# Second self-attention: one pass over both batches, fp32 scores of two heads in the two row halves of TensorE

## The reference, cut to what matters

```python
N_HEADS, D_HEAD = 16, 64
h = _layernorm(x, ln1_g, ln1_b)
q = (h @ sa_wq).reshape(B, S, 16, 64)
k = (h @ sa_wk).reshape(B, T, 16, 64)
v = (h @ sa_wv).reshape(B, T, 16, 64)
attn = softmax(einsum('bihd,bjhd->bhij', q, k) * 64 ** -0.5)
x = einsum('bhij,bjhd->bihd', attn, v).reshape(B, S, 1024) @ sa_wo + sa_bo + x
```

## Time and profile before

| | |
|---|---|
| Median of 3 runs | 2552.8 us (2549.9 to 2553.42) |
| The profiled execution, its own time | 2548.93 us |
| Its span, first to last instruction | 2547.2 us |
| Granted TensorE clock, mean over the span | 0.934 of full |
| TensorE busy | 2199.0 us (86%) |
| VectorE busy | 1323.1 us (52%) |
| ScalarE busy | 877.3 us (34%) |
| GpSimd busy | 501.7 us (20%) |
| Second self-attention with its projection, 941.9 to 1998.2 us | 1056.3 us |

### The profile page before, as it was taken

How to read it: one execution, slowest core, us unless ns; L and a number is a source line. 1 busy time by engine, 2 the same in 40 slices (tenths; PEclk the granted TensorE clock), 3 DMA queues, 4 the chain that set the end, 5 groups by cost and what they waited for, 6 DMA issues and landing times. The chain is left out here.

```text
span 2547.2 us, 27612 instructions
## 1 busy us (share of the span) xinstructions
PE 2199.0 (86%) x10154; PEld 1359.7 (53%) x10154; DVE 1323.1 (52%) x2139; ACT 877.3 (34%) x1349; POOL 501.7 (20%) x391
## 2 busy tenths in 40 slices
PE   5389997798999948999999989999998788898987
PEld 3234434386866834444444545444444677585766
DVE  4776652625244336666666256666664124535353
ACT  3046663322323222444444304444444132212221
POOL 3201100013123120332222202232323001202020
PEclk9699998799999977999999979999999799999989
DMA  3724302000000011000000011000000440000000
GB/s 110 112 34 52 44 12 77 15 1 1 1 0 0 1 31 40 24 24 23 23 24 18 1 37 39 24 23 23 23 17 1 117 117 1 0 9 8 0 9 8
DMA packets 62286, 71.34 MB, mean 28 GB/s; under 512 B 15386, under 2 KB 49180, under 8 KB 61892
## 3 DMA queue, kind: packets, MB, share of 16 engines
q1 hardware_dynamic: 62180, 69.92, 12.5%
HBM read 44.39 MB, written 8.73 MB: 21 GB/s over the span
## 5 line engine op out<-in xcount | busy, mean ns | idle before, releaser
L1694 DVE TENSOR_REDUCE pmax_b<-ring_b 128x1 f32<-128x512 f32 x512 | 346.7, 689 | 162.0 <-PE ring_b L1578 159.7
L1746 ACT ACTIVATE pr_b<-sc_b 128x1024 f32<-128x1024 f32 x256 | 261.7, 1023 | 352.8 <-PE sc_b L1598 352.8
L1656 POOL TENSOR_TENSOR sum_b<-sum_b,pr_b 128x1024 f32<-128x1024 f32 x96 | 228.3, 2378 | 247.3 <-ACT pr_b L1746 247.3
L1578 PE MATMUL ring_b<-k_hh_b,q_hl_b 128*128 128x512 f32 x512 | 241.2, 492 | 34.9 <-DVE pmax_b L1694 12.3
L1608 PE MATMUL o_b<-pr_b,v_b 128*64 128x512 f32 x1024 | 270.0, 617 | 0.0
L1578 PEld LDWEIGHTS ring_b<-k_hh_b,q_hl_b 128*128 128x128 f32 x512 | 102.2, 202 | 233.7 <-DVE pmax_b L1694 139.9
L504 ACT ACTIVATE probs<-s 128x512 f32<-128x512 f32 (+1 forms) x304 | 163.2, 575 | 159.8 <-PE s L414 112.9
L1596 PE MATMUL sc_b<-q_hl_b,k_hh_b 128*128 128x512 f32 x512 | 208.1, 406 | 4.7 <-ACT pr_b L1746 2.5
L1598 PE MATMUL sc_b<-q_m_b,k_l_b 65*128 65x512 f32 x512 | 204.8, 400 | 0.0
L982 PE MATMUL c_ps<-vw,c_pT 128*128 128x256 f32 x640 | 165.5, 419 | 22.2 <-ACT c_pT L1046 22.2
L982 PEld LDWEIGHTS c_ps<-vw,c_pT 128*128 128x128 f32 x640 | 132.6, 213 | 47.4 <-ACT c_pT L1046 25.4
(11 more groups left out here) (275 smaller groups left out, 3439.7 us busy)
## 6 DMA issues: line engine op xcount, KB each, us to landing
q_m_b<-q_hl_b SPq DMA_DIRECT2D x32, 256.0 KB, 3.5
k_hh_b<-k_hh_b SPq DMA_DIRECT2D x32, 256.0 KB, 3.4
qk_dram<-qk_parts SPq DMA_DIRECT2D x32, 192.0 KB, 2.8
q_stack<-qk_dram SPq DMA_DIRECT2D x48, 128.0 KB
k_stack<-qk_dram SPq DMA_DIRECT2D x48, 128.0 KB
x<-in_x SPq DMA_DIRECT2D x1, 2048.0 KB, 8.3
mlp_w<-in_L_xattn_mlp_w SPq DMA_DIRECT2D x2, 1024.0 KB, 8.5
wq_b<-in_L_xattn_sa_wq SPq DMA_DIRECT2D x16, 128.0 KB, 2.2
```

The costliest lines, as they stand in the source:

```text
L1578: te.matmul(ring[:, halves[i % 2]], q_hl[new][j][:, t * P:(t + 1) * P], k_hh[new][j][:, halves[half]], start=True, stop=True).then_inc(s1_ ...
L1656: engine.tensor_tensor(out=total[j][:], in0=other[:], in1=probs[j][kt % KEPT][:], op=ALU.add).then_inc(done, 1)
L1694: dve.tensor_reduce(part_max[:, half, j, t:t + 1], ring[:, halves[i % 2]], AX.X, ALU.max).then_inc(s1_max, 1)
L1746: act.activation(probs[j][kt % KEPT][:], s2[u % 2][:], ACT.Exp).then_inc(exp_made, 1)
```

## The change

`part_attention2` is called once and goes over 16 pairs, 8 of each batch, in one Block that holds the output projection too.

- **Scores.** A unit u = 8 * half + kt (0 to 15) is one tile of 128 keys, one half of 512 queries, and both heads. For each head there is a bf16 matmul (`picks` by `shift`) that puts the negated maximum into PSUM, and one fp32 matmul of contraction 64 (`kf` by `qf`). Head 0's operands lie on partitions 0 to 63, head 1's on 64 to 127. The splits of q and k and the DMA copies are gone. The maximum is carried as three bf16 parts (`split`, five small instructions of VectorE), and VectorE rounds q and k to F32R for the maxima (four casts a pair).
- **Maxima.** 32 F32R matmuls of contraction 64 a pair (`maxima`), heads in turn, in a ring of three PSUM tensors.
- **Order of TensorE.** Two units; then what `aside` gives for these two (projections in u = 0 to 2, four maxima for each u from 3 to 10, the turn at u = 11); then two steps of values, two units behind.
- **Sums.** All 14 additions of a pair are on GpSimd. The sums over partitions (`den`) use a slot of `s2`, twice a pair; ScalarE copies the values out (`copy_out`) and inverts (`invert`), in two halves.
- **Output projection.** Batch 0's eight tiles go behind units 12 to 15 of pairs 8 and 9 (`outs`), batch 1's behind the last pair. All weights are loaded at the start, in four chunks.

```diff
-def part_attention2(nc, e, A, b):
+def part_attention2(nc, e, A):
...
+        PAIRS, U, KEPT, SLOTS, CHUNKS, RING = 16, 16, 5, 12, 4, 3
+        S1 = 32
+        w = [sb(f"sa_w{n}", [P, KC, 1024]) for n in "qkv"]
+        wo_w, wo_brep = sb("wo_w", [P, 8, C]), sb("wo_brep", [P, C])
+        aT = sb("aT2", [P, SLOTS, T])
+        qf, kf = [sb(f"q_full{i}", [P, T]) for i in two], [sb(f"k_full{i}", [P, T]) for i in two]
+        qr, kr = sb("q_round", [P, T], F32R), sb("k_round", [P, T], F32R)
+        v = [sb(f"v_pair{i}", [P, TB, P]) for i in two]
+        probs = [sb(f"pr{i}", [P, 2, 512]) for i in range(KEPT)]
+        total, rden, raw = ([sb(f"{name}{h}", shape) for h in two] for name, shape in (
+            ("total", [P, 2, 512]), ("rden2_", [P, 512]), ("raw2_", [P, 512])))
+        part_max, row_max = sb("pmax", [P, 2, TB, 2]), sb("rmax", [P, 2, TB])
+        top, top_rest = sb("top2", [16, P]), sb("top2_rest", [16, P])
+        top_parts = [sb(f"top2_parts{i}", [16, 3, P], BF16) for i in two]
+        shift = [sb(f"shift{i}", [P, T], BF16) for i in two]
+        picks = sb("picks", [P, P], BF16)
+        ring = [ctx.enter_context(nc.psum_tensor(f"ring2_{i}", [P, 512], F32)) for i in range(RING)]
+        s2 = [ctx.enter_context(nc.psum_tensor(f"sc{i}", [P, 2, 512], F32)) for i in two]
+        o = ctx.enter_context(nc.psum_tensor("o2", [P, 512], F32))
...
+        head = (slice(0, 64), slice(64, P))
+        halves = (slice(0, 512), slice(512, T))
...
+        DEN_AT = 1
+        LAG = 2
...
+        def aside(u):
+            return (range(2 * u, 2 * u + 2) if u < 3 else (), range(4 * (u - 3), 4 * (u - 2)) if 3 <= u < 11 else (),
+                    u == 11)
+        def outs(n, u):
+            return (u - 12 + 4 * (n - 8),) if n in (8, 9) and u >= 12 else ()
...
+            for i in range(CHUNKS):
+                cols = slice(256 * i, 256 * i + 256)
+                for tile, n in zip(w, ("sa_wq", "sa_wk", "sa_wv")):
+                    sp.dma_start(tile[:, :, cols], A["L2_xattn_" + n].rearrange("(k p) f -> p k f", p=P)[:, :, cols]
+                                 ).then_inc(w_in[i], 16)
+            sp.dma_start(wo_w[:], A["L2_xattn_sa_wo"].rearrange("(k p) c -> p k c", p=P)).then_inc(wo_in, 16)
+            sp.dma_start(wo_brep[:], A["L2_xattn_sa_bo"].partition_broadcast(P)).then_inc(wo_in, 16)
...
+            for n in range(PAIRS):
+                sp.wait_ge(top_made, 5 * (n + 1))
+                sp.dma_start(e.top_dram[n % 2, :, 0:16].rearrange("s r q -> r s q"), top_parts[n % 2][:]
+                             ).then_inc(top_out, 16)
+                sp.wait_ge(top_out, 16 * (n + 1))
...
+                    sp.dma_start(shift[n % 2][64 * j:64 * j + 3], e.top_dram[n % 2, :, 8 * j:8 * j + 8].rearrange(
+                        "s t q -> s (t q)")).then_inc(shift_in, 16)
...
+            def project(n, i):
+                b, p, dst, half = n // 8, n % 8, ring[i % RING], i % 2
...
+                if i == 2 and n:
+                    te.wait_ge(top_made, 5 * (n - 1) + 1)
+                if i >= RING:
+                    te.wait_ge(kept, 6 * n + i - RING + 1)
...
+                if i < 4:
+                    for k in range(KC):
+                        ins = te.matmul(dst[:], w[i // 2][:, k, p * P:(p + 1) * P],
+                                        tokens_of(512 * half, 512 * half + 512)[:, k], start=k == 0, stop=k == KC - 1)
...
+            def maxima(n, i):
+                t, half, j = i // 4, i // 2 % 2, i % 2
+                if i < RING:
+                    te.wait_ge(kept, 6 * n + 4 + i)
+                    te.wait_ge(rounded, 4 * n + 4)
+                else:
+                    te.wait_ge(s1_free, S1 * n + i - RING + 1)
+                te.matmul(ring[i % RING][:], qr[head[j], t * P:(t + 1) * P], kr[head[j], halves[half]], start=True,
+                          stop=True).then_inc(s1_made, 1)
+            def turn(n):
+                te.wait_ge(max_made, n + 1)
+                te.transpose(ring[2][0:16, 0:P], row_max[:].rearrange("p j t -> p (j t)"), e.ident[:]
+                             ).then_inc(max_turned, 1)
+            def project_out(b, t):
+                if t >= 2:
+                    te.wait_ge(wo_added, 1 + 8 * b + t - 1)
+                for g in range(8):
+                    ins = te.matmul(ring[t % 2][:, 0:C], aT[:, (8 * b + g) % SLOTS, t * P:(t + 1) * P], wo_w[:, g, :],
+                                    start=g == 0, stop=g == 7)
+                ins.then_inc(wo_made, 1)
+            def unit(n, u):
+                half, kt = divmod(u, 8)
+                at = order_of(n, u)
+                if u == 0:
+                    te.wait_ge(shift_in, 32 * (n + 1))
+                if at >= 2:
+                    te.wait_ge(s2_free, at - 1)
+                keys = slice(kt * P, (kt + 1) * P)
+                for j in two:
+                    te.matmul(s2[at % 2][:, j], picks[head[j]], shift[n % 2][head[j], halves[half]], start=True,
+                              stop=False)
+                for j in two:
+                    ins = te.matmul(s2[at % 2][:, j], kf[n % 2][head[j], keys], qf[n % 2][head[j], halves[half]],
+                                    start=False, stop=True)
+                ins.then_inc(s2_made, 1)
+            def den(n, h):
+                at = den_order(n, h)
+                te.wait_ge(s2_free, at - 1)
+                te.wait_ge(sums, 7 * (2 * n + h + 1))
+                for j in two:
+                    ins = te.matmul(s2[at % 2][64 * j:64 * j + 64, 0], e.ones[:], total[h][:, j], start=True, stop=True)
+                ins.then_inc(s2_made, 1)
+            def values(n, u):
+                half, kt = divmod(u, 8)
+                te.wait_ge(s2_free, order_of(n, u) + 1)
+                if kt == 0 and (n or half):
+                    te.wait_ge(raw_made, 2 * n + half)
+                for j in two:
+                    ins = te.matmul(o[64 * j:64 * j + 64], v[n % 2][:, kt, 64 * j:64 * j + 64],
+                                    probs[(U * n + u) % KEPT][:, j], start=kt == 0, stop=kt == TB - 1)
+                ins.then_inc(pv_made, 1)
+            def behind(g):
+                if LAG <= g < U * PAIRS + LAG:
+                    values(*divmod(g - LAG, U))
+                n, u = divmod(g, U)
+                if u == 8 + DEN_AT and n < PAIRS:
+                    den(n, 0)
+                if u == DEN_AT and n:
+                    den(n - 1, 1)
+            for i in range(6):
+                project(0, i)
+            for i in range(S1):
+                maxima(0, i)
+            turn(0)
+            te.wait_ge(rows_set, 2)
+            te.wait_ge(shift_set, 2)
+            for n in range(PAIRS):
+                for first in range(0, U, 2):
+                    both = (first, first + 1)
+                    for u in both:
+                        unit(n, u)
+                    for u in both if n + 1 < PAIRS else ():
+                        for i in aside(u)[0]:
+                            project(n + 1, i)
+                    for u in both if n + 1 < PAIRS else ():
+                        for i in aside(u)[1]:
+                            maxima(n + 1, i)
+                    for u in both:
+                        behind(U * n + u)
+                    for u in both if n + 1 < PAIRS else ():
+                        if aside(u)[2]:
+                            turn(n + 1)
+                    for t in outs(n, first) + outs(n, first + 1):
+                        if t == 0:
+                            te.wait_ge(wo_in, 32)
+                            te.wait_ge(a_made, 16)
+                        project_out(0, t)
...
+            te.wait_ge(a_made, 2 * PAIRS)
+            for t in range(TB):
+                project_out(1, t)
...
+            for n in range(PAIRS):
+                for u in range(U):
+                    half, kt = divmod(u, 8)
...
+                    pool.tensor_tensor(out=total[half][:], in0=other[:], in1=probs[at % KEPT][:],
+                                       op=ALU.add).then_inc(sums, 1)
...
+            def rounding(n, i):
+                dve.wait_ge(kept, 6 * n + i + 1)
+                if n and i % 2 == 0:
+                    dve.wait_ge(s1_made, S1 * n)
+                dve.tensor_copy((qr, kr)[i // 2][:, halves[i % 2]], (qf, kf)[i // 2][n % 2][:, halves[i % 2]]
+                                ).then_inc(rounded, 1)
...
+            def maxima(n, i):
+                t, half, j = i // 4, i // 2 % 2, i % 2
+                dve.wait_ge(s1_made, S1 * n + i + 1)
+                dve.tensor_reduce(part_max[:, j, t, half:half + 1], ring[i % RING][:], AX.X,
+                                  ALU.max).then_inc(s1_free, 1)
...
+            def finish_maxima(n):
+                dve.wait_ge(s1_free, S1 * (n + 1))
+                if n:
+                    dve.wait_ge(max_turned, n)
+                dve.tensor_tensor(out=row_max[:], in0=part_max[:, :, :, 0], in1=part_max[:, :, :, 1],
```

(93 more changed lines are left out.)

373 lines of the change are left out of this document (99 added, 274 removed).

## The result

The kernel after takes 2633.1 us (median of four runs, 2625.6 to 2642.1) against 2552.2 us: a ratio of 1.032 (95% interval 1.030 to 1.034). The forecast was 2613 us, the range 2560 to 2720, the chance of slower 0.83. The profiled execution is the longest of the four, 2642.1 us with a span of 2640.0; it is 93 us over the profiled one of before.

A forecast was written before the change was run, and what follows sets the result against it. TensorE was taken as the bound, held by blocks of maxima paced by VectorE's reduces. Pairs +87, seam -32, start -3, end -7 and clock +15 gave +60: 2613 us against 2552.8, range 2560 to 2720.

The forecast's parts named there:

- What bounds the stage: Maxima on TensorE, second attention: blocks of eight 4.0 us, of four 1.5, 15.0 us a pair against 7.4 before.
- The chain 0.40 + 0.69 + 4 x 0.62 + 0.23 and 0.2 of handing over: Block of eight maxima: first matmul, first reduce, four reduce paces, last matmul and handing over, 4.0 us of TensorE.
- One sign that the prediction named for it: Trace after: TensorE idle before maxima, put down to the reduces, some 9 us a pair, starts 0.62 us apart.
- The unit: Scores on TensorE: row halves stream together, 1.09 us a unit, 17.4 us a pair; 2.18 if one after the other.
- the rival of partly overlapping halves: Row halves of a unit overlap only in part, 1.4 us a unit: +80, 2693 us; chance 0.09.
- a half-filled array streams fp32 faster: Rival for the scores: fp32 matmul filling half the rows streams in half the time, -110, 2503 us; chance 0.12.
- Changes of mode: TensorE between row halves and other work: eight a pair there and back at 0.34 us, 2.7 us.
- The clock: TensorE's granted clock falls after one in four of forty-five blocks of maxima, +15 us.
- the rival in which every block has a fall: Clock falls in every block of maxima: 63 us in place of 15, 2660 to 2680 us; chance 0.10.
- The last pair: End of the stage: double steps 34 us, last addition, Ln, Exp and division 8, projection 28; 70.5 against 77.2.
- The start and the seam: Start of the stage 49.5 us against 52.6, so -3; seam between the batches 91.7 against 124.2, so -32.
- Waits for Ln: Third unit after each sum over partitions waits for the slot that Ln reads: 0.8 us, twice a pair.

The follow-up runs named there:

- e8: Kernel after with both halves of a unit taking head 0's operands, on the same partitions 0 to 63: 2986.2 us in a single run.
- e4: Kernel after with the doubling of steps undone (one unit, its projections or four maxima, one step of values): 2546.8 us, 0.9987 of the kernel before.
- e1: Kernel after with maxima taken two or three at a time over the double step instead of in blocks of eight: 2487.5 us, 0.975 of the kernel before.
- e6: As e1 with the maxima placed earlier, 6, 9, 8, 8, 1 over five double steps instead of 6, 8, 7, 7, 4: 2474.9 us, 0.971 of the kernel before.
- e7: As e6, with v's projection between the two units of double step 2, 3: 2456.0 us, 0.963 of the kernel before.
- e9: Kernel after in single steps, two maxima after the unit and two after the step of values: 2445.5 us, 0.958 of the kernel before.
- e10: As e9, with VectorE making the seven additions of the last pair's second half in place of GpSimd: 2441.3 us, 0.957 of the kernel before.
- e2: Kernel after with the reduces of the maxima reading 256 of 512 columns: 2522.3 us, 111 less than the kernel after.
- e5: Kernel after with two slots in the ring instead of three: 2715.3 us, 82 more than the kernel after.
- e3: Kernel after with six of seven GpSimd additions in each half cut to 64 of 512 columns per head: 2623.3 us, 10 less than the kernel after.

## Why the prediction was right, and where its terms were off

**What bounds the stage.** Right. The blocks of maxima are the bound's new part: a block of eight holds TensorE for 4.0 us at full clock, as worked out, one of four for 1.6 (1.5 forecast), and spreading them takes 146 us off the kernel. The chain 0.40 + 0.69 + 4 x 0.62 + 0.23 and 0.2 of handing over stands; VectorE's pace was 0.60. One sign that the prediction named for it did not come: 9 us a pair of idle time before the maxima, put down to the reduces. The trace has 33.0 us in all, 2 a pair, because the records cover most of the waiting.

**The unit.** Right: 1.08 us against 1.09. The value taken from the column halves holds for the row halves, and e8 shows the other bound, 2.16. So the rival of partly overlapping halves falls, with its time of 2693 us. The estimate carried over from TensorE: Matmul & The Clock Gate of the Trainium skill (section "Measured speedup vs the span model"), 1.4 us, does not hold here; the measured 1.08 decides. That a half-filled array streams fp32 faster falls too: a record of contraction 64 takes 0.43 us alone (e8) as one of 128 does.

**Changes of mode.** Mis-sized: 0.24 us there and back, not 0.34, from e4. In the kernel before, the F32R pass behind the values takes 0.34 us to the next start and not 0.23 (1306.73 to 1307.07); the bf16 matmul that stands there in e4 takes 0.23 (1220.99 to 1221.22). Eight a pair, so 0.8 us a pair too much.

**The clock.** Mis-sized, and the largest error. I had one block in four causing a fall, +15 us. The profiled run after has half clock for 96 us of the time between pair 1's and pair 15's first projection, in 25 falls, and there are 42 blocks of eight in that time: more than one in two. Each of the 25 begins within a block of eight or in the values right behind one. The spell of 3.4 us at 1223.8 made the values 1.06 and the units behind 0.6 us longer, 1.6 us together; 28 times that (96 / 3.4) are 45 us. The pairs agree: with 3.4, 6.8 and 10.2 us at half clock they take about 64.7, 66.3 and 67.4 us. So the truth lay nearer to the rival in which every block has a fall, 63 us, than to my 15. The four runs differ by 16 us, and the two shorter ones have a mean clock of 0.934 and 0.935, the two longer 0.927 and 0.928, so the clock goes with the difference. The orders without blocks of eight (e1, e4, e6, e7, e9, e10), and the one with short reduces (e2), have no fall in these pairs, and e5, with longer blocks, has 147 us of half clock. What exactly makes one block in two escape is not shown.

**The last pair.** Mis-sized: 49.8 us to the output projection where I had 42. I had set GpSimd's 33.3 us beside TensorE's 34 and added the rest after them; but an addition takes 2.4 us and 0.15 to the next, TensorE waits 2.4 us for the first sum over partitions and 3.5 for the last, and ScalarE's two inversions lie on the path. e3, which nearly takes the additions away, brings these 49.8 us to 43.2, so the additions are 6.6 of the 7.8 us.

**The start and the seam.** The first unit came at 990.8 where I had 991.4, and that is luck. The terms of the start add up to 48.2 us, not to the 49.5 that the prediction states, and two of them were off in opposite ways: the first projection came 10.4 us in where I had 5, and the turn with the split and both DMAs took 5.3 where I had 9 with the cold clock. The projection of batch 0 costs 14.2 us in each of its two pairs, 28.4 in all (e9: 67.5 against 53.3), for 28.2.

**Waits for Ln.** 13.7 us in 27 waits, 0.5 each, where I had 0.8; but see e7, where more was gained than the waits that went.

**Sum.** In the profiled run: the pairs (1020.4 us with batch 0's 28.4) are 992 for fifteen, where I had 952.5 and 15 for the clock, so +24.5; the end +11 (49.8 + 31.4 for 70.5); the start 0. +60 becomes +95, against 94.3 measured in the stage of that run; by the medians it is +81. A pair without a fall would take about 63.2 us (an estimate, 64.7 less 1.5 for one spell), which is the 63.5 of the forecast within errors that partly cancel: 0.8 too much for the changes of mode and 0.6 for Ln against 0.2 too little for the blocks and some 0.9 that no item here accounts for.

## What to carry to other kernels

When one engine issues work in order and another frees the slots, the number of slots is how far it may run ahead, and a block longer than that costs the consumer's pace times what is beyond. Put no more such matmuls in one place than there are free slots, and give them streams of other work to lie under; here that alone was worth 146 us in double steps (e1) and 101 in single ones (e4 to e9), with the same instructions, and e9 is 188 us under the kernel after. Look for the cost at the block's two ends, since pipelined matmul records hide it in the idle column, and look at the granted clock behind the block, which may add to it.

## What the runs showed of the hardware that I had not expected

VectorE's casts wait for GpSimd. A cast of 16 x 128 elements to bf16 takes 0.21 us when GpSimd is idle and some 2 us when an addition is running there, and ends with it (minimum, median and maximum in ns, kernel after):

```profile
L1709 DVE CAST top_parts<-top x16: 214/1854/1862, 986.2 to 2003.1; 16x128 bf16<-16x128 f32 x16
...
L1713 DVE CAST top_parts<-top_rest x16: 214/2266/2270, 986.8 to 2005.3; 16x128 bf16<-16x128 f32 x16
```

With the additions cut short (e3) the same two casts take:

```profile
L1711 DVE CAST top_parts<-top x16: 214/214/215, 987.5 to 1991.8; 16x128 bf16<-16x128 f32 x16
...
L1715 DVE CAST top_parts<-top_rest x16: 214/214/216, 988.1 to 1992.4; 16x128 bf16<-16x128 f32 x16
```

The timeline of one turn in the kernel after shows that it is a wait for the whole of the other's instruction:

```profile
1369.56 4.85 POOL L1671 TENSOR_TENSOR total<-total,pr 128x1024 f32<-128x1024 f32 x2 [9.38 <-ACT pr L1810]
1370.71 1.24 DVE L1699 TENSOR_TENSOR rmax<-pmax 128x16 f32<-128x16 f32 x1
...
1372.63 1.85 DVE L1709 CAST top_parts<-top 16x128 bf16<-16x128 f32 x1
1374.52 0.28 DVE L1711 TENSOR_TENSOR top_rest<-top,top_parts 16x128 f32<-16x128 f32 x1
1374.62 2.41 POOL L1671 TENSOR_TENSOR total<-total,pr 128x1024 f32<-128x1024 f32 x1 [0.20 <-ACT pr L1810]
1374.84 2.27 DVE L1713 CAST top_parts<-top_rest 16x128 bf16<-16x128 f32 x1
```

Two additions run from 1369.56 to 1374.41; the first cast ends at 1374.48. The next addition ends at 1377.03, the second cast at 1377.11. The subtractions keep their 0.28 us: each begins just behind such an end, at 1374.52 and 1377.14, ahead of the next addition (1374.62 and 1377.17). The wait goes the other way too: the addition at 1377.17 takes 3.07 us in place of some 2.4, while VectorE multiplies for `aT` from 1377.35 to 1378.02. Where an operation with two inputs does meet an addition it waits as the casts do: `rmax`, 0.24 us long in e3, takes 1.24 and ends with the first addition. By SBUF — State Buffer of the Trainium skill (section "SBUF: two separate sides"), the ports that the two engines share are locked for a whole instruction by whichever starts first, an instruction of GpSimd or one of VectorE that uses both ports or has two inputs in SBUF, and the other engine waits; the trace agrees. The forecast left it out of the turn: the five small steps take 5.1 us where I had 1.3. That costs TensorE little. Between the pairs it waits 10.4 us for `rmax` at the turn (15 times) and 1.4 for the maxima's DMA (3 times), and with the additions cut short (e3) for neither; the longest wait for that DMA, 4.9 us, is in the start, when GpSimd is idle.

Two row halves start within some ns of each other and hold their pace of 0.43 us a record, the weight loads of 0.19 us each included.
